# Reordering SyncE's work within a step, and rounding the keys' rest in an earlier slot of ScalarE

## The reference

```python
x = x + cross_attention(ctx, layernorm(x))      # 16 heads, 32 half-heads of 8 features
x = x + moe(layernorm(x))                       # 16 experts, 2 chosen for each token, and a shared one
```

## Time and profile before

| | us |
|---|---|
| median of three timed runs (2256.3 to 2265.62) | 2256.83 |
| the profiled execution | 2249.22 |
| its span, first to last instruction | 2247.5 |
| TensorE busy | 2021.7 |
| VectorE busy | 1584.5 |
| ScalarE busy | 1426.2 |
| GpSimd busy | 1446.2 |

### The profile page before, as it was taken

How to read it: one execution, slowest core, us unless ns; L and a number is a source line. 1 busy time by engine, 2 the same in 40 slices (tenths; PEclk the granted TensorE clock), 3 DMA queues, 4 the chain that set the end, 5 groups by cost and what they waited for, 6 DMA issues and landing times.

```text
span 2247.5 us, 76469 instructions
## 1 busy us (share of the span) xinstructions
PE 2021.7 (90%) x20840; PEld 1405.2 (63%) x20840; DVE 1584.5 (71%) x4623; ACT 1426.2 (63%) x3511; POOL 1446.2 (64%) x2183
## 2 busy tenths in 40 slices
PE   4999999999999999999999999999977988889996
PEld 3666665566656566656656566666546877768775
DVE  3777777777777777778777777778765655546554
ACT  2777777777777777777776777777763444434443
POOL 4466777767677676767676767767664555545554
PEclk8899999999999999999999999999987999999999
DMA  5997777777777777777777777878846777667774
GB/s 133 222 225 192 187 195 190 178 189 184 191 190 184 186 194 185 185 183 182 191 193 178 184 188 190 194 181 216 228 173 180 223 214 214 199 178 220 220 223 127
DMA packets 616921, 432.05 MB, mean 192 GB/s; under 512 B 447811, under 2 KB 562634, under 8 KB 616400
## 3 DMA queue, kind: packets, MB, share of 16 engines
q1 hardware_dynamic: 556528, 319.91, 58.3%
q0 software_dynamic: 32256, 84.47, 11.8%
q10 hardware_dynamic: 28000, 26.03, 3.8%
HBM read 234.59 MB, written 197.72 MB: 192 GB/s over the span
## 4 chain that ended last, share of the span: by engine, by line
PE 67%; DVE 15%; issue 10%; ACT 3%; DMA 2%; SPq 1%; POOL 1%; DVEq 1%; another core or an unknown queue 1%; ACTq 0%; POOLq 0%
PE mx_ps L494 11%; PE o_ps L527 7%; DVE mx L982 6%; PE ms_ps L778 5%; PE o_ps L538 5%; PE ms_ps L555 5%; PE mx_ps L557 4%; PE mx_ps L555 4%; PE ms_ps L576 4%; PE st_ps L756 3%; PE mx_ps L556 3%; PE ms_ps L583 3%; PE st_ps L487 3%; PE ms_ps L556 3%; PE ms_ps L557 2%
## 5 line engine op out<-in xcount | busy, mean ns | idle before, releaser
L982 DVE TENSOR_REDUCE mx<-mx_ps 128x4 f32<-128x512 f32 x1024 | 686.3, 685 | 300.4 <-PE mx_ps L494 294.2
L826 ACT ACTIVATE prob<-st_ps 128x512 f32<-128x512 f32 x1024 | 604.5, 598 | 357.8 <-PE st_ps L487 353.5
L494 PE MATMUL mx_ps<-stacks 48*128 48x128 bf16 x4096 | 396.7, 221 | 67.6 <-DVE mx L982 33.8
L487 PE MATMUL st_ps<-stacks 50*128 50x128 bf16 x4096 | 394.9, 220 | 0.0
L494 PEld LDWEIGHTS mx_ps<-stacks 48*128 48x128 bf16 x4096 | 230.9, 95 | 228.6 <-issue 105.9
L527 PE MATMUL o_ps<-prob,v_sb 128*32 128x256 f32 x4096 | 331.6, 396 | 0.8 <-ACT prob L826 0.4
L1344 POOL DMA_INDIRECT rows_dram<-rowt,posi x256 | 253.7, 991 | 67.6 <-issue 64.3
L555 PE MATMUL ms_ps<-e_lo 128*128 128x256 f32 x768 | 264.7, 345 | 18.1 <-issue 11.1
L923 ACT ACTIVATE rows_T<-st_ps 128x256 fp32r<-128x256 f32 x288 | 111.7, 388 | 192.2 <-PE st_ps L756 137.3
L487 PEld LDWEIGHTS st_ps<-stacks 50*128 50x128 bf16 x4096 | 229.8, 95 | 2.5 <-issue 1.5
L1413 POOL DMA_INDIRECT sums_dram<-stacks x144 | 141.7, 984 | 130.4 <-DVE stacks L1220 70.2
(11 more groups left out here) (155 smaller groups left out, 4694.4 us busy)
## 6 DMA issues: line engine op xcount, KB each, us to landing
stack_dram<-w_dn_sb SPq DMA_DIRECT2D x768, 128.0 KB
stacks<-stack_dram SPq DMA_DIRECT2D x512, 192.0 KB
stacks<-rows_dram SPq DMA_DIRECT2D x288, 130.0 KB
w_dn_sb<-in_x SPq DMA_DIRECT2D x64, 256.0 KB
w_dn_sb<-in_ctxT SPq DMA_DIRECT2D x64, 256.0 KB
x_res<-in_x SPq DMA_DIRECT2D x64, 256.0 KB
stacks<-sums_dram SPq DMA_DIRECT2D x78, 128.0 KB
stacks<-base_dram SPq DMA_DIRECT2D x76, 128.0 KB
```

The source lines that it names most:

```text
L487: return pe.matmul(st_ps[k % 2][:, i * P:(i + 1) * P], k_st[p][64 * h:64 * h + KROWS, u, j, :], q_st[p][64 * h:64 * h + KROWS, u, j, :], s ...
L494: return pe.matmul(mx_ps[k % 2][:, i * P:(i + 1) * P], q_st[p][64 * h:64 * h + ROWS, u, j, :], k_st[p][64 * h:64 * h + ROWS, u, j, :], sta ...
L826: nc.scalar.activation(prob[k % 4][:, :], st_ps[k % 2][:, :], ACT.Exp, scale=float(HALF) ** -0.5).then_inc(a_exp, 1)
L982: v.tensor_reduce(mx[:, u, c * CHUNK:(c + 1) * CHUNK], mx_ps[k % 2][:, :].rearrange("p (c n) -> p c n", c=CHUNK), AX.X, ALU.max).then_inc( ...
```

## The change

No operation is added or removed. On SyncE the three later Q copies now go with the first three, ahead of the second half's maxima; the load of the residual's input `x_res` moves from the end of the step to a place behind the K copies; both halves of the first stacks are read in one go ahead of the first half's maxima; and the load of the next context `c_in` goes behind these maxima. On ScalarE the rounding of the keys' rest moves from slot 4 to slot 2. On GpSimd the split of the keys moves ahead of the norm's terms.

```diff
@@ SyncE, step @@
                 if n2.is_in(0, NS):
                     wait(sp, g_qs, 1, n2, 1)
-                    put_parts(n2, 0, qp, d_qw, Q_COPIES, range(PARTS))
+                    put_parts(n2, 0, qp, d_qw, Q_COPIES, range(COPIES))
                 if it.is_in(0, NS):
                     put_max(it, 1)
                 if n2.is_in(0, NS):
-                    put_parts(n2, 0, qp, d_qw, Q_COPIES, range(PARTS, COPIES))
                     wait(sp, g_ks, 1, n2, 1)
                     put_parts(n2, 1, kp, d_kw, K_COPIES, range(COPIES))
-                if xs.is_in(1, NS):
-                    wait(sp, g_cl, 1, xs)
-                    sp.dma_start(c_in[:, :, :],
...
+                if b.is_in(0, NS):
+                    wait(sp, g_x2, 4, it, 0)
+                    sp.dma_start(x_res[1 - p][:, :, :],
...
                     load_stacks(n2, 0, 1)
+                    load_stacks(n2, 0, 0)
                 if b.is_in(0, NS):
                     put_max(b, 0)
-                if n2.is_in(0, NS):
-                    load_stacks(n2, 0, 0)
-                if b.is_in(0, NS):
-                    wait(sp, g_x2, 4, it, 0)
-                    sp.dma_start(x_res[1 - p][:, :, :],
...
+                if xs.is_in(1, NS):
+                    wait(sp, g_cl, 1, xs)
+                    sp.dma_start(c_in[:, :, :],
...
@@ ScalarE, step @@
                     if k == 2 and do_c:
                         copy_max(it, 1)
+                    if k == 2 and do_k:
+                        wait(act, g_kr, 1, k2, 1)
+                        nc.scalar.activation(kp[:, 1, :], k_rest[:, :], ACT.Copy).then_inc(a_kb, 1)
...
-                    if k == 4 and do_k:
-                        wait(act, g_kr, 1, k2, 1)
-                        nc.scalar.activation(kp[:, 1, :], k_rest[:, :], ACT.Copy).then_inc(a_kb, 1)
@@ GpSimd, step @@
                 if do_d:
                     residual(d, 2)
+                if do_k:
+                    split(k2, k_rest, kp, a_kb, g_ks)
                 if do_xs:
                     norm_terms(xs, mv1, nb1, ve1, v_s1, g_ve1, g_r1, g_nb1)
-                if do_k:
-                    split(k2, k_rest, kp, a_kb, g_ks)
```

More of the change, by code:

```diff
@@ L401, in step @@
                 if n2.is_in(0, NS):
-                    put_parts(n2, 0, qp, d_qw, Q_COPIES, range(PARTS, COPIES))
                     wait(sp, g_ks, 1, n2, 1)
                     put_parts(n2, 1, kp, d_kw, K_COPIES, range(COPIES))
-                if xs.is_in(1, NS):
-                    wait(sp, g_cl, 1, xs)
-                    sp.dma_start(c_in[:, :, :],
-                                 ctxT[bass.ds(xs.idx(), 1)].rearrange("g p k t -> (g p) k t")).then_inc(d_c, 16)
+                if b.is_in(0, NS):
+                    wait(sp, g_x2, 4, it, 0)
+                    sp.dma_start(x_res[1 - p][:, :, :],
+                                 x_g[bass.ds(b.idx(), 1)].rearrange("g p u d -> (g p) u d")).then_inc(d_res[1 - p], 16)
                 if n2.is_in(0, NS):
@@ L416, in step @@
                     load_stacks(n2, 0, 1)
+                    load_stacks(n2, 0, 0)
                 if b.is_in(0, NS):
                     put_max(b, 0)
-                if n2.is_in(0, NS):
-                    load_stacks(n2, 0, 0)
-                if b.is_in(0, NS):
-                    wait(sp, g_x2, 4, it, 0)
-                    sp.dma_start(x_res[1 - p][:, :, :],
-                                 x_g[bass.ds(b.idx(), 1)].rearrange("g p u d -> (g p) u d")).then_inc(d_res[1 - p], 16)
+                if xs.is_in(1, NS):
+                    wait(sp, g_cl, 1, xs)
+                    sp.dma_start(c_in[:, :, :],
+                                 ctxT[bass.ds(xs.idx(), 1)].rearrange("g p k t -> (g p) k t")).then_inc(d_c, 16)
                 if xs.plus(1).is_in(1, NS):
```

## The result

The changed kernel takes 2408.55 us (median of 4 runs, 2404.27 to 2420.8), the kernel before 2258.78 in the same comparison: ratio 1.0667, 95% interval 1.0619 to 1.0714. That is slower, as forecast, but by 150 us and not by 60, and outside the range. The profiled execution has a span of 2404.1 us and a mean granted clock of 0.928; before it was 0.972.

What follows compares the result with a forecast made beforehand. TensorE, 93% busy in the loop, was taken as the bound, with ScalarE's slots 2 and 3 setting the step. 60 us for the rounding and 0 for the rest gave 2309, as median 2317 us; range 2280 to 2340.

Steps and rivals of the forecast that it cites:

- The moved rounding on ScalarE: Slot 2: ScalarE waits for GpSimd's key_rest, delaying exponential, v_sb and routing product 1.00 us a step, 60 us in all.
- Split and SyncE's order: GpSimd's split ahead of the norm's terms and SyncE's reordered copies and loads: value 0 each.
- The sum: 60 - 0 - 0 = 60 us on the profiled 2249.2 us; as a median 2317 us, 2.7% slower.
- the three slips: Three steps where GpSimd idles longer ahead of key_rest, at some 3 us: 9 us more, kept for the range only.
- the 31 us kept as its low end: Lower bound of the rounding's cost: if GpSimd came early enough, only the rounding's 0.52 us a step would be left.
- The rivals: Alternatives: only the rounding's length lost, 2288 us (0.13); delay absorbed (0.06); GpSimd pacing, 2222 us (0.04); late maxima, 2377 us (0.03).
- Slower still: Rival: second half's maxima, behind six copies on SyncE, come late for slot 8; 2377 us, chance 0.03.
- What would show it: Signs: ScalarE waits in slot 2, v_sb wait about 1.6 us, TensorE busy 90%, steps 26.3 us, tile stage unchanged.
- What bounds the kernel: In the loop: TensorE 93% busy, waiting 0.6 us a step for ScalarE's v_sb copy ahead of the routing product.

Runs made afterwards that it cites:

- e1: The kernel before with ScalarE's edit alone, the rounding of the keys' rest in slot 2: 2409.44 us, ratio 1.0705.
- e2: The changed kernel with the rounding put back into slot 4, SyncE's and GpSimd's new order kept: 2251.54 us, ratio 1.0006.
- e5: The changed kernel with two repeated gate_up(1) products, results unused, ahead of the routing product in slot 3: 2317.09 us, ratio 1.0306.
- e9: The kernel before, with GpSimd forming the keys' rest at the end of the step before, between two pairs of row scatters: 2191.59 us, ratio 0.9763.
- e11: The kernel before, with GpSimd's residual moved behind the four row scatters, which then run without a pause: 2417.78 us, ratio 1.079.
- e4: The changed kernel with one repeated gate_up(1) product, result unused, ahead of the routing product in slot 3: 2348.57 us, ratio 1.0422.
- e12: The kernel before, with the keys' rest formed early and all four row scatters held apart by GpSimd's existing work: 2168.98 us, ratio 0.958.

## Why the prediction was right in its direction and wrong in its size

- **The moved rounding on ScalarE, 60 us.** Right, as place, mechanism and size: 1.04 us a step without a fall (there are 7 of them) against the forecast 1.00, the wait for v_sb 1.66 a step against 1.6, and e1 and e2 put the whole loss on this edit. ScalarE's wait in the changed kernel is longer than the 0.4 to 0.5 us that the text named as a minimum, 1.22 in the mean: part of it takes the place of waiting that ScalarE did before anyway.
- **Split and SyncE's order, 0 each.** Right: e2 has both and a ratio of 1.0006 (0.9978 to 1.0035).
- **The sum.** Here it failed. It has a term for the delay and none for the clock. The text read "at a granted clock of 0.99" off and carried it over unsaid to a kernel whose TensorE would stand still for 1.6 us in each step instead of 0.6. The missing term is most of the 84.6 us, out of 137.5, in the 51 steps counted; the 7 us of the three slips in it are what the text had put into its range. e5 measured the sum without it: a ratio of 1.0306, where the sum said 2.7% (e5's own work is included, and its comparison had a faster kernel before, so that its 2317.09 us agree with the forecast 2317 to the microsecond is luck). The range of the forecast itself, 2295 to 2337, has a small slip too: the 31 us kept as its low end give 2288.
- **The rivals.** "Slower still" had the right side and the wrong mechanism: SyncE's order did nothing, and its 2377 would have fallen short too. No rival put a price on the clock.
- **What would show it.** The step of 26.3 us was found in the few steps without a fall only. The busy share fell to 90%, as forecast, but that agrees for a wrong reason: slow matmuls count as busy.
- **What bounds the kernel.** The chain's link from v_sb to the routing product was read rightly, but its cause was put down to the order of slots 2 and 3 alone. e9 shows that most of that 0.6 us was the late signals beneath it, which no term of the prediction had.

## What to carry to other kernels

Before adding a wait to an engine that TensorE depends on, ask how long TensorE will then stand still there, in one piece (the changed kernel) or in several close together (e11): beside the wait itself, the clock may fall, and here that cost more than the wait. A cheap test of it is to fill the gap with work whose result nobody reads; if the kernel gets faster and the granted clock in the profile rises with it, as in e4 and e5, the clock is the reason, and then look for useful work to put there, or better, for what causes the gap. And read the start of an instruction against the end of what it waited for: where the two lie 1 us apart with an idle engine between, look at what the other engines do in that time.

## What the hardware showed that was not expected

**TensorE's signals come late while GpSimd issues row scatters.** From 300 to 1500 us of the kernel before I set the semaphore updates recorded in the trace against the ends of the matmuls that make them. Within reach of a row scatter (0.3 us before it to 0.7 us after it) 571 of 842 came over 0.3 us late, of the base rows' scatters 82 of 292, and elsewhere none of 1830. (The ends are modelled, and where two updates fall together the matching can be off, so these are counts and no more.) By themselves they don't single TensorE out: counted in the same way, 130 of 397 updates of ScalarE and 152 of 530 of VectorE come over 0.3 us late at the row scatters too, and others have no record near.

The starts of the engines that waited tell more. Of ScalarE's instructions that a matmul released whose end lies within 0.3 us of a row scatter, 68 of 69 started over 0.4 us after that end, of VectorE's 40 of 47; released by matmuls elsewhere, none of 244 and none of 143. In the same places TensorE started at most 0.07 us after the instruction of VectorE that released it (56 times) and 0.13 us after that of ScalarE (15 times). So signals of VectorE and ScalarE are not held there, and TensorE's are. In e12, with pauses, ScalarE started so late 12 times of 91 at the row scatters and VectorE 9 of 72, and ScalarE 17 of 244 elsewhere.

The matmuls themselves aren't slower, what waits for them is: at the upper clock the 608 of line 527 that run beside a row scatter take 392 ns in the mean, the other 2360 take 391. e9, e11 and e12 only move GpSimd's instructions among each other and span ratios from 0.958 to 1.079. The Trainium skill (page "SBUF — State Buffer", section "SBUF: two separate sides") says that TensorE never waits on anyone at SBUF's ports, and of DMAs that GpSimd issues it tells only how VectorE can hold them up. That is not contradicted, as the matmuls run on, but a reader who takes GpSimd's scatters for harmless to what waits for TensorE would be wrong here. By what path they hold the signals back, no run here shows.

**More work, less time.** Adding 2.1 us of useless matmuls to each step took 91 us off the changed kernel (e5 against 2408.55; some 80 by the ratios), because TensorE then kept its higher clock in most steps (4 falls in 51 instead of 44).
